# Packed words for TensorE's reads of the tile table in a mixture-of-experts stage, and a weight column in a ring of eight

## The reference, cut to what matters

```
topk_w, topk_idx = route(x, w_router, b_router)    # 8 of 64 experts per token, 8192 tokens
g = ragged_dot(x_sorted, we_gate, group_sizes)     # 512 x 256 per expert
u = ragged_dot(x_sorted, we_up, group_sizes)       # 512 x 256
o = ragged_dot(silu(g) * u, we_down, group_sizes)  # 256 x 512
y = zeros.at[tok].add(o * w_sorted[:, None]) + shared(x)
```

## Time and profile before

| | |
|---|---|
| median of 3 runs | 3972.36 us (3971.4 to 3972.74) |
| profiled execution | 3973.47 us, span 3971.7 us |
| TensorE busy | 3650.4 us (92%) |
| VectorE busy | 2313.6 us (58%) |
| GpSimd busy | 1602.0 us (40%) |
| ScalarE busy | 1349.9 us (34%) |
| chain that ended last | TensorE 59%, VectorE 5%, "issue" 5% |
| costliest lines of the chain | L1437 34%, L1456 16%, L1407 5%, L1579 3%, L1466 3% |

### The profile page before, as it was taken

The page is one execution under the profiler, slowest core; times in us unless marked ns, Lnnn a source line. Parts: engine busy times, 40 slices in busy tenths (PEclk is TensorE's granted clock), DMA queues, the critical chain, the costliest instruction groups (busy, mean ns, idle before and its releaser), DMA issues.

```text
span 3971.7 us, 110141 instructions
## 1 busy us (share of the span) xinstructions
PE 3650.4 (92%) x16856; PEld 2774.8 (70%) x16857; DVE 2313.6 (58%) x5802; ACT 1349.9 (34%) x4031; POOL 1602.0 (40%) x1208
## 2 busy tenths in 40 slices
PE   6809999967999999999999999999999999999996
PEld 3404445536877777787778778787888777787785
DVE  5364555555666665656665565656555666666653
ACT  2212222213333433434333343334333343334331
POOL 1010000004555555555555455555555555455443
PEclk9959999988999999999999999999999999999998
DMA  3322323225666676667666666666666676666654
GB/s 113 106 61 86 98 97 98 96 56 122 125 154 149 153 155 122 149 127 167 141 134 127 158 137 124 138 139 152 124 127 140 122 169 153 140 133 154 137 102 74
DMA packets 216177, 502.40 MB, mean 126 GB/s; under 512 B 46587, under 2 KB 46715, under 8 KB 215360
## 3 DMA queue, kind: packets, MB, share of 16 engines
q0 software_dynamic: 129024, 320.94, 43.4%
q1 hardware_dynamic: 86592, 177.77, 13.6%
q10 hardware_dynamic: 512, 3.15, 0.3%
HBM read 1115.65 MB, written 191.41 MB: 329 GB/s over the span
## 4 chain that ended last, share of the span: by engine, by line
PE 59%; DVE 5%; issue 5%; DVEq 2%; ACT 2%; DMA 2%; ACTq 1%; POOLq 0%; POOL 0%; SPq 0%
PE e_ps_gu L1437 34%; PE e_ps_y L1456 16%; PE e_ps_x L1407 5%; DVE e_w_low L1579 3%; PE e_ps_h L1466 3%; ACT e_w_high L1516 2%; DMA out<-e_y,e_y_ids 2%; PE e_ps_find L1419 1%; DVEq L1301 1%; ACTq L1301 1%; DVE e_past L1611 1%; DVE e_y L1606 1%; DVE e_below L1622 0%; DVEq L1579 0%; ACT e_silu L1535 0%
## 5 line engine op out<-in xcount | busy, mean ns | idle before, releaser
L1381 POOL DMA_INDIRECT out<-e_y,e_y_ids x576 | 935.9, 1625 | 1326.5 <-ACT e_weight L1528 582.4
L1373 POOL DMA_INDIRECT e_x<-token_rows,e_x_ids x576 | 615.9, 1069 | 273.5 <-issue 172.7
L1437 PE MATMUL e_ps_gu<-e_w_high,e_xT_high 128*128 x2304 | 688.4, 419 | 15.1 <-issue 5.1
L1437 PE MATMUL e_ps_gu<-e_w_low,e_xT_high 128*128 x2304 | 646.6, 399 | 6.4 <-issue 4.8
L1437 PE MATMUL e_ps_gu<-e_w_high,e_xT_low 128*128 x2304 | 650.4, 401 | 0.2 <-issue 0.2
L1606 DVE TENSOR_SCALAR e_y<-e_ps_y,e_weight 128x512 f32 (+1 forms) x576 | 430.9, 748 | 243.6 <-PE e_ps_y L1456 202.9
L1587 DVE TENSOR_TENSOR e_xT_low<-e_ps_x,e_xT_high 128x512 fp32r<-128x512 f32 x576 | 397.7, 690 | 286.9 <-ACT e_xT_high L1524 173.6
L1437 PEld LDWEIGHTS e_ps_gu<-e_w_high,e_xT_low 128*128 128x128 f32 x2304 | 428.8, 189 | 128.1 <-issue 29.2
L1437 PEld LDWEIGHTS e_ps_gu<-e_w_low,e_xT_high 128*128 128x128 f32 x2304 | 428.8, 188 | 126.5 <-issue 31.1
L1535 ACT ACTIVATE e_silu<-e_ps_gu 128x256 f32<-128x256 f32 x576 | 221.2, 384 | 821.5 <-PE e_ps_gu L1437 627.0
L1437 PEld LDWEIGHTS e_ps_gu<-e_w_high,e_xT_high 128*128 128x128 f32 x2304 | 396.2, 191 | 98.1 <-issue 37.3
(11 more groups left out here) (245 smaller groups left out, 3926.0 us busy)
## 6 DMA issues: line engine op xcount, KB each, us to landing
e_w_raw<-in_L_ffn_we_gate SPq DMA_DIRECT2D x576, 512.0 KB
e_w_raw<-in_L_ffn_we_up SPq DMA_DIRECT2D x576, 512.0 KB
e_w_raw<-in_L_ffn_we_down SPq DMA_DIRECT2D x576, 512.0 KB
a_x<-in_L_attn_x SPq DMA_DIRECT2D x64, 256.0 KB, 3.4
t_x_in<-in_L_attn_x SPq DMA_DIRECT2D x64, 256.0 KB, 2.8
token_rows<-t_xn SPq DMA_DIRECT2D x64, 256.0 KB, 3.1
out<-t_y_out SPq DMA_DIRECT2D x64, 256.0 KB, 2.0
e_x<-token_rows,e_x_ids POOLq DMA_INDIRECT x576
```

The costliest lines, as they stand in the source:

```text
L1373: pool.indirect_dma_start(x[:, s % XS, :], None, k.rows, bass.IndirectOffsetOnAxis(x_ids[:, s:s + 1], 0)) \
L1381: pool.indirect_dma_start(k.out, bass.IndirectOffsetOnAxis(y_ids[:, s:s + 1], 0), y[:, s % YS, :], None, compute_op=ALU.add).then_inc(adde ...
L1437: last = nc.tensor.matmul(ps_gu[s % 2][:], x[:, s % 2, c, :], w[:, c], start=(n == 0), stop=(n == 3 * DC - 1))
```

## The change

There are three parts.

(1) tile_table() also makes packed words. VectorE copies place and expert of each tile as numbers into pairs; SyncE stores them to a new table in memory and reads them back into one row. VectorE then computes, on one partition, one number of eight places in base 4 for each eight tiles, and one of four experts in base 64 for each four tiles, and writes both into k.packed. These steps stand behind the last work that VectorE had in the stage.

(2) TensorE no longer loads words from k.tiles. It loads one packed word of places for each eight tiles at the head of step s == 0 (ahead of turn_x), the word of the eight tiles before in the same step after the third matmul of gate_up, and one packed word of experts for each four tiles. place_of(s) takes the tile's place out of the register by a division by a power of four and a mask, when gate_up and when down begin; expert_of(t) does the same for the expert's number.

(3) The column of routing weights is one of eight: ScalarE and VectorE address it by the slot of the ring, a register, and ScalarE waits for y_made of eight tiles ago instead of four.

```diff
+            nc.vector.tensor_copy(pairs[:, :, 0], place[:])
+            nc.vector.tensor_copy(pairs[:, :, 1], expert[:])
             nc.vector.scalar_tensor_tensor(out=table[:, :, 2], in0=freed[:], scalar=1.0, in1=reused[:],
                                            op0=ALU.add, op1=ALU.add)
             v.drain().then_inc(made, 1)
...
+            v.wait_ge(pairs_stored, 32)
+            for t in range(UNROLL - 2, 0, -1):
+                nc.vector.scalar_tensor_tensor(
+                    out=places[:], in0=by_eight[:, :, UNROLL - 1, 0] if t == UNROLL - 2 else places[:],
+                    scalar=float(WSLOTS), in1=by_eight[:, :, t, 0], op0=ALU.mult, op1=ALU.add)
+                if t >= SHORT:
+                    nc.vector.scalar_tensor_tensor(
+                        out=experts[:], in0=by_four[:, :, SHORT - 1, 1] if t == UNROLL - 2 else experts[:],
+                        scalar=float(E), in1=by_four[:, :, t - SHORT, 1], op0=ALU.mult, op1=ALU.add)
+                v.drain()
+            nc.vector.scalar_tensor_tensor(out=packed_eight[:, :, 0], in0=places[:], scalar=float(WSLOTS),
+                                           in1=by_eight[:, :, 0, 0], op0=ALU.mult, op1=ALU.add)
+            nc.vector.tensor_copy(packed_four[:, :, 1], experts[:])
...
             sp.wait_ge(made, 1)
+            sp.dma_start(k.pairs.rearrange("(q p) f -> p q f", p=P), pairs[:]).then_inc(pairs_stored, 16)
             sp.dma_start(k.table.rearrange("(q p) f -> p q f", p=P), table[:]).then_inc(stored, 16)
+            sp.wait_ge(pairs_stored, 16)
+            sp.dma_start(pairs_row[:], k.pairs.unsqueeze(0)).then_inc(pairs_stored, 16)
...
-            words = Words(pe)
+            places = [None, None]
+            found_in = [None]
+            held = [None] * SHORT
+
+            def packed(i, most):
+                return pe.value_load(k.packed[0:1, bass.ds(i, 1)], min_val=0, max_val=most)
+
+            def place_of(s):
+                return pe.snap((places[0 if s >= 0 else 1] // WSLOTS ** (s % UNROLL)) & (WSLOTS - 1))
...
-            def expert_of(i):
-                return pe.snap(entry(pe, i, 0, 2 * WSLOTS * E - 1) // (2 * WSLOTS), min_val=0, max_val=E - 1)
+            def expert_of(t):
+                return pe.snap((found_in[0] // E ** t) & (E - 1), min_val=0, max_val=E - 1)
...
-                place = words.place(s)
+                place = place_of(s)
...
-                if third == 1 and s + 1 < UNROLL:
-                    words.load(i + 1, s + 1)
-                if s == 0 and third == 0:
-                    words.load(i - 2, s - 2)
-                if s == 0 and third == 2:
-                    words.load(i - 1, s - 1)
-                if s % SHORT in (1, 2) and third != 1:
-                    t = 2 * (s % SHORT - 1) + third // 2
-                    if exists(i - s % SHORT + AHEAD_FIND + t):
-                        held[t] = expert_of(i - s % SHORT + AHEAD_FIND + t)
+                if s == 0 and third == 0 and exists(i - UNROLL):
+                    places[1] = packed(i - UNROLL, WSLOTS ** UNROLL - 1)
+                if not exists(i - s % SHORT + AHEAD_FIND):
+                    return
+                if s % SHORT == 1 and third == 1:
+                    found_in[0] = packed(i - s % SHORT + AHEAD_FIND + 1, E ** SHORT - 1)
+                if s % SHORT == 2 and third != 1:
+                    for t in (third, third + 1):
+                        held[t] = expert_of(t)
 
             def step(i, s):
+                if s == 0:
+                    places[0] = packed(i, WSLOTS ** UNROLL - 1)
                 if exists(i + 1):
                     turn_x(i + 1, (s + 1) % UNROLL)
-                if s == 0:
-                    words.load(i, s)
...
-                after(act, y_made, i - SHORT + 1)
-                nc.scalar.copy(weight[:, s % SHORT:s % SHORT + 1],
+                after(act, y_made, i - UNROLL + 1)
+                nc.scalar.copy(weight[:, bass.ds(slot, 1)],
...
                 nc.vector.tensor_scalar(y[:, bass.ds(slot, 1), :].rearrange("p o d -> p (o d)"), ps_y[s % 2][:],
-                                        weight[:, s % SHORT:s % SHORT + 1], None, ALU.mult).then_inc(y_made, 1)
+                                        weight[:, bass.ds(slot, 1)], None, ALU.mult).then_inc(y_made, 1)
```

More of the change, by code:

```diff
@@ L1067, in tile_table @@
         table = sb("table", [P, Q, 3], I32)
+        pairs = sb("pairs", [P, Q, 2])
+        pairs_row = sb("pairs_row", [1, TABLE, 2])
+        places = sb("places", [1, TABLE // UNROLL])
+        experts = sb("experts", [1, TABLE // SHORT])
         ends = sb("ends", [E, 1])
@@ L1084, in tile_table @@
         stored = ctx.enter_context(nc.semaphore("q_stored"))
+        pairs_stored = ctx.enter_context(nc.semaphore("q_pairs_stored"))
         totalled = ctx.enter_context(nc.semaphore("q_totalled"))
@@ L1170, in _ @@
                 nc.vector.tensor_tensor(k.rank[:, at:to], k.rank_row[:, at:to], ps_first[i][:, 0:to - at], ALU.subtract)
+            by_eight = pairs_row[:].rearrange("o (m s) f -> o m s f", s=UNROLL)
+            by_four = pairs_row[:].rearrange("o (m s) f -> o m s f", s=SHORT)
+            packed_eight = k.packed[:].rearrange("o (m s) -> o m s", s=UNROLL)
+            packed_four = k.packed[:].rearrange("o (m s) -> o m s", s=SHORT)
+            v.wait_ge(pairs_stored, 32)
[11 more added lines that the diff above has]
+            nc.vector.tensor_copy(packed_four[:, :, 1], experts[:])
         @block.tensor
@@ L1224, in expert_tiles @@
         x = sb("x", [P, XS, ROW])
-        weight = sb("weight", [P, SHORT])
+        weight = sb("weight", [P, UNROLL])
         xT_high = sb("xT_high", [P, 2, DC, P], F32R)
@@ L1493, in step @@
                 if exists(i - 2):
-                    down(i - 2, (s - 2) % UNROLL)
-            held = [None] * SHORT
+                    down(i - 2, s - 2)
             for i in range(0, AHEAD_FIND, SHORT):
-                find(i, [expert_of(i + t) for t in range(SHORT)])
+                found_in[0] = packed(i + 1, E ** SHORT - 1)
+                find(i, [expert_of(t) for t in range(SHORT)])
             turn_x(0, 0)
@@ L1692, in program @@
         k.counts = nc.dram_tensor("rank_counts", [NB, E, P], BF16).ap()
+        k.pairs = nc.dram_tensor("tile_pairs", [(TILES // P + 1) * P, 2], F32).ap()
         k.table = nc.dram_tensor("tile_table", [(TILES // P + 1) * P, 3], I32).ap()
@@ L1701, in program @@
         k.tiles = sb("tiles", [1, TABLE * 3], I32)
+        k.packed = sb("packed", [1, TABLE], I32)
         with ExitStack() as early:
```

## The result

The changed kernel takes 4025.11 us (median, 4024.04 to 4030.18) beside 3972.55 us for the kernel before on the same chip: ratio 1.0131, 95% interval 1.0114 to 1.0149. It is slower by 52.6 us. The forecast was 3965.6 us; the time also lies above its range. The profiled execution took 4030.18 us, 56.7 more than that of before, and the traces are compared by it.

The account below looks back on a forecast made before the run. TensorE was taken to bound the kernel. Terms -17 + 3.4 + 4.3 + 2.5 = -6.8 us took the profiled 3973.5 us to 3966.7, and 1.1 less gave a median of 3965.6 us; range 3952 to 3976 us.

Parts of the forecast that it names:

- The account of late loads: TensorE's table-word loads cost time only after a wait; removing them saves 17 us, bounds 0 and 44.
- new experts at place 1: Tiles with number modulo 4 equal to 1: 6.01 us falls to 5.2 or less, saving 7 us over nine.
- The steps at places 0 and 1: Tiles by number modulo 4: fewer late loads save 7.5 us at 0, 7 at 1, 2.5 more at 1.
- the excess: Expert-stage time above TensorE's undisturbed steps, 110.4 of 3009.84 us; only this can be won unless the step falls.
- The slack: Between e_past's end and the next find, new expert at 1 modulo 4: 1.5 us shrinks to about 0.5.
- 34 x 0.1 = 3.4 us: Added place_of() register work on TensorE, unhidden at 34 finds that waited: 3.4 us, bounds 0 and 7.
- Place 2: New expert at tile number modulo 4 equal to 2: dropped loads only lengthen the find's e_past wait; gain 0.
- The ring: VectorE's register address lengthens chains to e_past and w_low: 4.3 us, bounds 0 and 8; ScalarE's shorter wait gains 0.
- rival (c): e_past comes earlier with TensorE, or ScalarE's shorter wait brings splits forward: 19 us more won, 3947 us; chance 0.09.
- The gapless chain: VectorE's work from a split's down part to e_past has only its own gaps, so TensorE's lateness doesn't touch it.
- 17 - 3.4 - 4.3 - 2.5: Late loads removed, less TensorE register work, VectorE's longer chain and the longer start: net 6.8 us faster.
- (b): VectorE's backlog after a split takes back the gains, leaving the added 10.2 us: 3982 us; chance 0.08.

Follow-up runs that it names:

- eager: The changed kernel with each expert number's division and mask done ahead, when read, and kept in four registers; ratio 0.9998 to the kernel before, 3978.29 us.
- late_before: The kernel before, with VectorE doing the down part of the split twice where the new expert's tile number modulo 4 is 2; ratio 1.0096.
- ring_only: The kernel before with only the third part of the change, eight routing-weight columns instead of four; ratio 0.9976.

## Why the prediction was wrong

The account of late loads was right in kind: loads 288 (forecast 290); at nine of ten new experts at place 1 the tile takes 4.99 to 5.01 us (forecast 5.2 or less) and the find does not wait; the undisturbed steps are 4.91, 5.42 and 4.94 us; the first gate matmul stands at 921.34 (forecast 921). The steps at places 0 and 1 became shorter by 22.7 us, 17 forecast (in the table's columns, 25.5 less in gate_up and 4.6 more of waits). There are 142 finds in the stage and not 141, which moves the excess by half a microsecond. TensorE and VectorE at tile 189, to the earlier trace rows:

```profile
1930.40 1.18 PE L1476 MATMUL e_ps_gu<-e_w_high,e_xT_high 128*128 x4 [0.28 <-DVEq L1620]
...
1935.40 1.17 PE L1476 MATMUL e_ps_gu<-e_w_high,e_xT_high 128*128 x4
...
1940.49 0.89 PE L1458 MATMUL e_ps_find<-ranks,e_past 64*128 x4
1941.59 1.20 PE L1476 MATMUL e_ps_gu<-e_w_high,e_xT_high 128*128 x4 [0.21 <-issue]
```

```profile
1939.20 0.68 DVE L1649 TENSOR_TENSOR e_past<-slot_row,begin 64x512 bf16<-64x512 f32 x1 [0.63 <-issue]
```

The slack between e_past's end at 1939.88 and the find is 0.61 us, as forecast (about 0.5), and the find doesn't wait. But the stream has no lead there: from the first find matmul to the gate matmul it takes 1.10 us instead of the 0.33 of the earlier trace rows. The prediction had put 0.3 us aside for this at each of nine tiles; it is some 0.8. Four steps failed.

1. "34 x 0.1 = 3.4 us", the register work that isn't hidden. I counted place_of() and left expert_of() out, taking its division and mask as done in read_ahead where they are written. They are issued behind the wait. The term measured 38.3 us: 0.62 us more at each of the 34 finds that wait, and some 17 us at 21 finds that don't wait but come with an emptied stream, all of them the next find behind a new expert at place 1 (nine) or 0 (twelve). These 21 finds alone take back most of the 22.7 us won at places 0 and 1. Eager takes 36.1 of the 38.3 away. This step failed first, and without it the change is neutral (0.9998).

2. Place 2: "TensorE arrives 1.08 us earlier and waits 1.08 us longer. Gain 0". The exchange took place: loads -19.7, wait +22.5. But the wait is not free: the clock is granted at 1.2 GHz behind it, 23 times instead of 2, and gate_up behind the find lost 35.2 us. Half of that needs the sparse finds as well (eager: 22.3 left), half comes from the wait alone, as late_before shows without any of the change. The trace of before had one case: behind a find's wait of 2.66 us at tile 254, gate_up lost 1.53 us. Its waits of 1.81 and 2.00 us, at tiles 74 and 178, cost nothing of the kind, and I looked for none.

3. The ring: forecast +4.3 us, measured -0.24% and -0.28%, some 10 us the other way. The chain that was to grow by 0.1 us with the register address is the same in ring_only, 9.04 us, so this part of the term measured nothing. I put the gain of ScalarE's shorter wait at 0, with 5 us as the bound, although rival (c) named the mechanism.

4. The gapless chain in the earlier trace rows is not fixed: VectorE's load ahead of it took 0.78 instead of 0.31 us at tile 54 and over 0.7 us at all 18 such tiles, some 7 us in all, which are part of the 22.5 of step 2.

By the trace: 17 - 3.4 - 4.3 - 2.5 was the sum; 22.7 - 2.8 - 38.3 - 36.7 - 2.9 is what happened (the shorter steps at places 0 and 1; the exchange at place 2; the finds; the whole step behind them, 35.2 of it in gate_up; the start), a loss of 58 us, of which 1.2 came back behind the stage. The ring's gain is inside these terms. Of the rivals (b), with a chance of 0.08, had the sign, 3982 us, but neither mechanism nor price. Each of the first two steps alone carries the time beyond the range. The upper bound of the register term, 7 us, was much too low: the trace of before has one register instruction for each of four finds, and without lead they cost 0.5 us together; I didn't ask how many each find would have.

## What to carry to other kernels

Find the place in the stream where a computed register value is really evaluated; an expression written ahead of a wait but first used behind it costs its time behind it, where nothing hides it, and a register move ahead of the wait is the cure. When a change moves small losses of TensorE into one wait, price the matmuls behind the wait at 1.2 GHz as well. First remove the wait that others' lateness ends in (here one producer moved one step earlier, worth 0.75% with the old loads, from 0.9976 to 0.9901, and 2.8% with the packed words, from 1.0131 to 0.9852), then shorten the stream; in this kernel the shorter stream bought nothing in the other order (eager, 0.9998).

## What the hardware showed that was not expected

Waits of 1.66 us (late_before) and 1.87 us (changed kernel) at tile 54 were followed by 1.2 GHz for most of a gate_up (0.62 and 0.61 granted), one of 1.76 us (eager) was not; nor was every long wait of one kernel. Longer waits and sparser finds make it more frequent, and the two seem to count together: in the changed kernel four of the 22 slow gate_ups stand behind waits of only 0.51 to 0.93 us (tiles 82, 142, 218 and 490), while with close finds the shortest wait ahead of one was 1.16 us (ring_only, tile 178; 1.27 in late_before, 1.69 in eager). What decides a single case is not shown. The same load of a word into a register of VectorE took 305 or 780 ns at the same place of the program, the slow one almost always in the kernels with both the ring and packed places; TensorE's packed loads are 317 ns at the median and up to 1166.
